# Self attention: where the next head group's transposes stand, and how its projections are spread

## The chip, the cores and the metric

The kernel runs on one core of a Trainium2 chip. Its time is that of one execution on the device in microseconds (us), as the median of several runs. A core has five engines that run their own instruction streams and wait for each other through semaphores: TensorE (matmuls, PE in the profile, with its weight loads as PEld), VectorE (DVE), ScalarE (ACT), GpSimd (POOL) and SyncE (SP, which issues DMAs here).

## The reference

A decoder block in float32 with x of shape (4, 512, 512): self attention with 16 heads of 32 and rotary embedding, cross attention to a masked context of 1601 rows, and a mixture of 16 experts with 4 chosen per token beside a shared one. Each of the three is added to its input and layer normalised. The change lies in the first:

```
q, k, v = (proj(Wq), proj(Wk), proj(Wv))          # (B, 16 heads, 512, 32)
q = q * cos + _rotate_half(q) * sin
k = k * cos + _rotate_half(k) * sin
att = jnp.einsum('bhqd,bhkd->bhqk', q, k) / math.sqrt(hd)
mask = jnp.triu(jnp.full((T, T), -jnp.inf, dtype=att.dtype), k=1)
att = jax.nn.softmax(att + mask, axis=-1)
out = jnp.einsum('bhqk,bhkd->bhqd', att, v)
out = out.transpose(0, 2, 1, 3).reshape(B, T, D)
return out @ Wo.T
```

## The kernel before

Everything in self attention is written out by hand, engine by engine, with semaphores. The work comes in 16 head groups (counter g): 4 batches times 4 groups of 4 heads. Matmuls keep near float32 accuracy by splitting each operand into a high part in the fast fp32r format and a low part, the difference; a product is then three passes, or the two parts are stacked along the contraction.

One group g on TensorE, in this order:

1. Transposes (L519): 32 of them turn the rotated query and key parts of 4 heads into `proj_ps`, 4 for each of 8 halves (query and key of head 0, of head 1, ...). `proj_ps` has 4 banks, so from the fifth half on they wait for copies of earlier ones. ScalarE copies the query halves to `q_st` (L257), VectorE the key halves to `k_st` (L378).
2. Scores, in 8 steps of two heads (L471, and L473 which adds the causal mask); VectorE takes the row maximum of each (L387). Two PSUM banks hold scores, so a score waits for the maximum of the one two before it. Behind each step stand 5 of the 48 matmuls that project x for the next group (L438). In the first group of a batch the output projection of the batch before follows (L453, 48 matmuls).
3. 4 more projections, the transposes of the negative maxima (L540), and the last 4 projections. ScalarE and VectorE copy the maxima to `q_st` (L270, L407) as further rows of the contraction.
4. Transposed scores (L487), again in 2 banks, from which ScalarE takes the exponentials into `p_t` (L278). There are 4 blocks of keys (kc) with 4 heads each. GpSimd zeroes the masked half of each diagonal square (L202), and the values (L494) and weight sums (L501) of a block follow, interleaved with the next block's transposed scores. The last block's values and sums have nothing behind which to stand.

Beside part 4 VectorE rotates the next group's queries and keys once all its projections are done. It multiplies by cosines (L317) and sines (L320) and adds (L324), first for queries and then for keys. Then it copies the key's high part (L330), the values (L333), and subtracts for the low part (L335). ScalarE writes the query's high part behind the tenth exponential (L242), GpSimd its low part behind the third block's masks (L191). VectorE finishes the output of group g - 1 between the first maxima of g (L346 to L360), and ScalarE and GpSimd split it (L249, L195).

The weights of the output projection arrive in the buffer `rows` and are split once: ScalarE's `hi_wo` (L236) stands behind group 0's exponentials, VectorE's part (L304) behind its rotation for group 1. SP loads the residual `rows` over them when that is done. Nothing of cross attention or the experts starts before self attention has ended.

Of the kernel before, what the change touches and what calls it, by code (L numbers as in the profile page):

```python
# [40 lines left out]
TT = T // P  # L41
# [19 lines left out]
def self_attention(nc, sem, rows, xT, x, wqkvT, woT, rope, gather_x1):  # L61


    with ExitStack() as ctx:
# [82 lines left out]
        def groups(body):  # L147
            for b in range(B):
                for hg in range(HG):
                    body(b, hg, b == 0 and hg == 0, b == B - 1 and hg == HG - 1)  # L150

        with nc.Block() as block:
# [71 lines left out]
            @block.scalar  # L224
            def _(act):
                def hi_x(b, i):
                    if b >= 1:
                        act.wait_ge(x_in, b * 16)
                        act.wait_ge(projected, (b * HG - 1) * TT + i + 1)
                    src, hi, _ = x_places(b, i)  # L230
                    nc.scalar.activation(hi, src, ACT.Copy).then_inc(x_hi, 1)

                def hi_wo():
                    src, hi, _ = wo_places()
                    act.wait_ge(wo_in, 16)
                    nc.scalar.activation(hi, src, ACT.Copy).then_inc(w_hi, 1)  # L236

                def hi_q(g):
                    act.wait_ge(roped, g * 6 + 3)
                    act.wait_ge(turned, g * 2 * GH)  # L240
                    src, two_hi, _, _ = split_places(0)
                    nc.scalar.activation(two_hi, twice(src), ACT.Copy).then_inc(q_hi, 1)  # L242

                def hi_out(g, hg):

                    act.wait_ge(o_scaled, g + 1)
                    if hg == 0:
                        act.wait_ge(out_proj, g)
                    nc.scalar.activation(o_sp[:, 0, hg, :], o_f[:, :], ACT.Copy).then_inc(o_hi, 1)  # L249

                def group(b, hg, first, last):
                    g = b * HG + hg

                    act.wait_ge(scored_t, g * GH * TT)
                    for h in range(GH):
                        act.wait_ge(turned, g * 2 * GH + 2 * h + 1)
                        nc.scalar.activation(q_st[0:3 * HD, h, :], proj_ps[0:3 * HD, 2 * h % 4, :],  # L257
                                             ACT.Copy).then_inc(q_stacked, 1)
                    if hg == HG - 1 and not last:
                        hi_x(b + 1, 2)  # L260
                        hi_x(b + 1, 3)
                    if not first:
                        hi_out(g - 1, (hg - 1) % HG)
                    if hg == HG - 2 and b < B - 1:
                        hi_x(b + 1, 0)
                        hi_x(b + 1, 1)

                    act.wait_ge(max_turned, g + 1)
                    for h in range(0, GH, 2):
                        nc.scalar.activation(q_st[3 * HD:P, h, :], den_ps[32 * h:32 * h + 32, :],  # L270
                                             ACT.Copy).then_inc(max_stacked_a, 1)
                    act.wait_ge(summed, g)
                    for kc in range(TT):
                        w = T - kc * P
                        for h in range(GH):
                            n = kc * GH + h
                            act.wait_ge(scored_t, g * GH * TT + n + 1)
                            nc.scalar.activation(p_t[:, h, p_at[kc]:p_at[kc] + w],  # L278
                                                 score_ps[:, n % 2, kc * P:T], ACT.Exp,
                                                 scale=float(HD) ** -0.5).then_inc(exped, 1)  # L280
                            if n == 2 * GH + 1 and not last:
                                hi_q(g + 1)
                    if g == 0:
                        hi_wo()

                for c in range(DC):
                    act.wait_ge(chunk_in[c], 32)
                    hi_x(0, c)
                    src, hi, _ = w_places(c)
                    nc.scalar.activation(hi, src, ACT.Copy).then_inc(w_hi, 1)  # L290
                hi_q(0)
                groups(group)
                hi_out(NG - 1, HG - 1)

# [128 lines left out]
            def _(pe):  # L423
# [52 lines left out]
                def scores_t(g, kc, half):  # L476

                    q0 = min(kc * P, T - 2 * P)
                    for h in range(2 * half, 2 * half + 2):
                        n = kc * GH + h  # L480
                        if kc == 0 and h % 2 == 0:
                            pe.wait_ge(max_stacked_a, g * (GH // 2) + h // 2 + 1)
                        if kc == 0 and h % 2 == 1:
                            pe.wait_ge(max_stacked_v, g * (GH // 2) + h // 2 + 1)
                        if n >= 2:
                            pe.wait_ge(exped, g * GH * TT + n - 1)
                        nc.tensor.matmul(score_ps[:, n % 2, q0:T], k_st[:, h, kc * P:(kc + 1) * P],  # L487
                                         q_st[:, h, q0:T], start=True, stop=True).then_inc(scored_t, 1)
# [14 lines left out]
                                              start=(kc == 0), stop=(kc == TT - 1))  # L503
                    return mm

                def group(b, hg, first, last):
                    g = b * HG + hg

                    pe.wait_ge(q_lo, g + 1)
                    pe.wait_ge(roped, g * 6 + 5)  # L510
# [10 lines left out]
                                                     ident_r[:, :])  # L521
                        mm.then_inc(turned, 1)

                    STEP = 5
                    for n in range(2 * TT):
                        scores(g, n // 2, n % 2)
                        if not last:
                            project(g + 1, (hg + 1) % HG, n * STEP, (n + 1) * STEP)
                    if hg == 0 and not first:
                        project_out(b - 1)  # L530
                    at = 2 * TT * STEP
                    if not last:
                        project(g + 1, (hg + 1) % HG, at, at + 4)

                    pe.wait_ge(max_lo, g + 1)
                    if hg == 0 and not first:
# [3 lines left out]
                        mm = nc.tensor.transpose(den_ps[:, qt * P:(qt + 1) * P].bitcast(F32R),  # L540
                                                 neg_max[:, qt, :, :].rearrange("p h n -> p (h n)"), ident_r[:, :])
                    mm.then_inc(max_turned, 1)
                    if not last:
                        project(g + 1, (hg + 1) % HG, at + 4, len(products))
                    pe.wait_ge(maxed, g * GH * TT + GH * TT)
                    scores_t(g, 0, 0)
                    scores_t(g, 0, 1)
                    for kc in range(1, TT):
                        scores_t(g, kc, 0)
                        values(g, hg, kc - 1)  # L550
                        scores_t(g, kc, 1)
                        weight_sums(g, kc - 1)
                    values(g, hg, TT - 1)
                    weight_sums(g, TT - 1).then_inc(summed, 1)

                pe.wait_ge(const_ready, 3)
                project(0, 0, 0, len(products))
                groups(group)
                project_out(B - 1)

# [1393 lines left out]
```

## Time and profile before

| | us |
|---|---|
| median of 3 runs | 1554.73 (1553.87 to 1555.04) |
| the profiled execution | 1557.65 |
| its span, first to last instruction | 1555.9 |
| TensorE, weight loads busy | 1388.5, 1139.0 |
| VectorE busy | 1015.6 |
| ScalarE, GpSimd busy | 645.2, 334.8 |

The profile is of one execution; sums made with its durations are compared with its own time. "Granted clock" (PEclk) is TensorE's clock as a share of 2.4 GHz; it is 1.00 or 0.50 at any time, and values between are means over a stretch. "Idle before" in brackets is how long the engine stood before an instruction, with what released it.

### The profile page before, as it was taken

What the parts mean: (1) busy time and instruction counts of PE and PEld (TensorE: products, weight loads), DVE (VectorE), ACT (ScalarE), POOL (GpSimd) and SP (SyncE); (2) the same over time, 40 slices, a digit from 0 to 9 for tenths busy, and PEclk for the clock granted to TensorE, in tenths of its full rate; (3) what the DMA queues carried; (4) which work ended last, traced back from release to release, by engine and by line L of the source; (5) the groups of instructions that cost most, each with busy time, mean ns of one, the idle gap of its engine ahead of it and who ended that gap; (6) DMA issues with size and microseconds to landing.
All of it is one profiled execution on the core that took longest, in us unless ns stands there. A gap on an engine that the chain in (4) does not pass through costs nothing. (4 is left out here: it accounts for less than half of the span.)

```text
span 1555.9 us, 24568 instructions
## 1 busy us (share of the span) xinstructions
PE 1388.5 (89%) x8837; PEld 1139.0 (73%) x8837; DVE 1015.6 (65%) x1701; ACT 645.2 (41%) x1033; POOL 334.8 (22%) x491
## 2 busy tenths in 40 slices
PE   5999999999998679999999964699999999998990
PEld 5657666675665368888888854699999999997770
DVE  6767575577667275564654269677777777774777
ACT  3443244234243242423333142566565665663222
POOL 0242133123122210010100000322222222222562
PEclk9999999999998779999999985799999999998995
DMA  4200000000000131222220040677788777884563
GB/s 176 109 1 28 1 1 28 1 1 1 1 1 1 49 123 61 83 88 82 88 83 24 1 150 1 252 288 270 283 281 287 284 281 280 280 283 150 168 185 140
DMA packets 62024, 190.34 MB, mean 122 GB/s; under 512 B 7160, under 2 KB 7164, under 8 KB 61184
## 3 DMA queue, kind: packets, MB, share of 16 engines
q1 hardware_dynamic: 49312, 147.93, 26.5%
q0 software_dynamic: 12640, 41.43, 8.8%
q8 instruction: 48, 0.79, 0.2%
q14 instruction: 24, 0.20, 0.0%
HBM read 156.30 MB, written 33.03 MB: 122 GB/s over the span
## 5 line engine op out<-in xcount | busy, mean ns | idle before, releaser
L1527 DVE TENSOR_TENSOR e_w_sp<-e_w_raw,e_w_sp 128x1024 fp32r<-128x1024 f32 x141 | 168.6, 1221 | 17.9 <-ACT e_w_sp L1485 11.6
L438 PE MATMUL proj_ps<-wqkv,x_sp 128*128 128x384 f32 x768 | 170.9, 355 | 10.5 <-DVE wqkv L304 10.5
L1471 POOL DMA_INDIRECT e_x_g<-x_rows,e_index x94 | 101.3, 1078 | 321.7 <-DVE e_index L1538 307.1
L984 PE MATMUL c_score_ps<-ct,x_t 128*128 128x402 f32 x768 | 159.0, 359 | 0.0
L1485 ACT ACTIVATE e_w_sp<-e_w_raw 128x1024 fp32r<-128x1024 f32 x141 | 145.3, 1058 | 14.5 <-DMA e_w_raw<-w_experts 14.3
L1003 PE MATMUL c_out_ps<-cr,weigh_t 128*128 128x512 f32 (+1 forms) x624 | 147.3, 394 | 1.4 <-DVE weigh_t L843 1.4
L984 PEld LDWEIGHTS c_score_ps<-ct,x_t 128*128 128x128 f32 x768 | 140.6, 193 | 7.1 <-issue 5.3
L1586 PEld LDWEIGHTS e_gate_ps<-e_x_t,e_w_sp 128*128 128x128 f32 x1128 | 139.5, 190 | 5.9 <-DVE e_x_t L1548 1.8
L1586 PE MATMUL e_up_ps<-e_x_t,e_w_sp 128*128 128x256 f32 x1128 | 143.3, 283 | 0.0
L1586 PE MATMUL e_gate_ps<-e_x_t,e_w_sp 128*128 128x256 f32 x1128 | 141.0, 281 | 1.4 <-DVE e_x_t L1548 1.4
L438 PEld LDWEIGHTS proj_ps<-wqkv,x_sp 128*128 128x128 f32 x768 | 131.3, 194 | 11.1 <-issue 10.8
L1612 PE MATMUL e_down_ps<-e_w_sp,e_h_sp 128*128 128x512 f32 x564 | 139.0, 396 | 0.0
L387 DVE TENSOR_REDUCE row_max<-score_ps 128x1 f32<-128x128 f32 (+3 forms) x256 | 114.4, 485 | 34.8 <-PE score_ps L473 33.8
L1003 PEld LDWEIGHTS c_out_ps<-cr,weigh_t 128*128 128x128 f32 (+1 forms) x624 | 116.1, 188 | 26.2 <-issue 1.7
L1586 PEld LDWEIGHTS e_up_ps<-e_x_t,e_w_sp 128*128 128x128 f32 x1128 | 135.0, 188 | 0.0
L202 POOL TENSOR_SCALAR_AFFINE_SELECT p_t<-p_t 128x128 f32<-128x128 f32 x256 | 80.9, 328 | 216.1 <-ACT p_t L278 213.8
L278 ACT ACTIVATE p_t<-score_ps 128x512 f32<-128x512 f32 (+3 forms) x256 | 100.2, 437 | 51.2 <-PE score_ps L487 49.1
L1612 PEld LDWEIGHTS e_down_ps<-e_w_sp,e_h_sp 128*128 128x128 f32 x564 | 102.5, 188 | 21.4
L487 PEld LDWEIGHTS score_ps<-q_st,k_st 128*128 128x128 f32 x256 | 43.2, 194 | 96.9 <-ACT p_t L278 63.9
L487 PE MATMUL score_ps<-q_st,k_st 128*128 128x256 f32 (+2 forms) x256 | 86.6, 401 | 14.4 <-ACT p_t L278 12.7
L378 DVE CAST k_st<-proj_ps 96x512 fp32r<-96x512 f32 x64 | 40.8, 682 | 88.4 <-PE proj_ps L519 88.2
L784 ACT ACTIVATE weigh_t<-c_turn_ps 128x512 fp32r<-128x512 f32 x64 | 31.3, 515 | 134.4 <-PE c_turn_ps L959 134.4
(205 smaller groups left out, 2231.8 us busy)
## 6 DMA issues: line engine op xcount, KB each, us to landing
e_w_raw<-w_experts SPq DMA_DIRECT2D x141, 512.0 KB, 5.6
y_rows<-e_y SPq DMA_DIRECT2D x47, 512.0 KB, 3.1
raw<-ctxT SPq DMA_DIRECT2D x16, 800.5 KB, 4.3
raw<-ctx_rows SPq DMA_DIRECT2D x16, 768.0 KB, 4.9
rows<-x_rows SPq DMA_DIRECT2D x1, 4096.0 KB, 12.2
x_rows<-rows SPq DMA_DIRECT2D x4, 1024.0 KB, 5.9
out<-rows SPq DMA_DIRECT2D x4, 1024.0 KB, 5.2
rows<-wqkvT SPq DMA_DIRECT2D x4, 768.0 KB, 7.3
```

Of the source, the lines that this page charges most:

```text
L202: nc.gpsimd.affine_select(out=block_of, in_=block_of, compare_op=ALU.is_ge, fill=0.0, base=0, pattern=[[1, P]], channel_multiplier=-1).the ...
L278: nc.scalar.activation(p_t[:, h, p_at[kc]:p_at[kc] + w], score_ps[:, n % 2, kc * P:T], ACT.Exp, scale=float(HD) ** -0.5).then_inc(exped, 1)
L387: nc.vector.tensor_reduce(row_max[:, qt, h:h + 1], score_ps[:, n % 2, 0:(qt + 1) * P], AX, ALU.max).then_inc(maxed, 1)
L438: mm = nc.tensor.matmul(proj_ps[:, tt, 0:GW], x_sp[:, xs, c, tt * P:(tt + 1) * P], wqkv[:, ws, c, hg * GW:(hg + 1) * GW], start=(c == 0 an ...
L487: nc.tensor.matmul(score_ps[:, n % 2, q0:T], k_st[:, h, kc * P:(kc + 1) * P], q_st[:, h, q0:T], start=True, stop=True).then_inc(scored_t, 1)
L984: mm = nc.tensor.matmul(score_ps[:, f, 0:MQ], x1_t[:, xs, c, qt * P:(qt + 1) * P], ct[:, cs, c, f * MQ:(f + 1) * MQ], start=False, stop=(c ...
L1003: mm = nc.tensor.matmul(out_ps[:, n % 2, :], weigh_t[0:k, ws, c, :], cr[0:k, cs, c, :], start=(c == 0 and m == 0), stop=(c == MC - 1 and m ...
L1471: nc.gpsimd.indirect_dma_start(x_g[:, par, half, :], None, x2_rows, bass.IndirectOffsetOnAxis(ap=index[:, par, half:half + 1], axis=0)).th ...
L1485: nc.scalar.activation(w_sp[:, par, part, 0, :], w_raw[:, par, part, :], ACT.Copy).then_inc(w_hi[part], 1)
L1527: nc.vector.tensor_tensor(w_sp[:, par, part, 1, :], w_raw[:, par, part, :], w_sp[:, par, part, 0, :].bitcast(F32), ALU.subtract).then_inc( ...
L1586: mm = nc.tensor.matmul(ps[:, par, i, :], w_sp[:, par, part, ws, at:at + P], x_t[:, par, xs, c, :], start=(c == 0 and n == 0), stop=(c == ...
L1612: mm = nc.tensor.matmul(down_ps[:, half, :], h_sp[:, par, hs, i, half * P:(half + 1) * P], w_sp[:, par, DOWN, ws, i * D:(i + 1) * D], star ...
```

## The change

On TensorE the transposes of a group become a function of their own. It is called once ahead of group 0, and then for group g + 1 ahead of the last block's values of group g instead of at the start of g + 1. The 48 projections are spread anew: 5, 5, 4, 4, 4, 5, 4, 5 behind the eight score steps instead of 5 behind each; 4 ahead of the transposes of the maxima and 4 behind them, as before; and 4 between the first and the second pair of transposed scores. On ScalarE, `hi_wo` moves from the end of group 0 to behind its query copies. No instruction is added or removed.

```diff
@@ ScalarE, group @@
+                    if g == 0:
+                        hi_wo()
                     if not first:
                         hi_out(g - 1, (hg - 1) % HG)
...
-                    if g == 0:
-                        hi_wo()
@@ TensorE @@
-                def group(b, hg, first, last):
-                    g = b * HG + hg
+                def turn_heads(g):
                     pe.wait_ge(q_lo, g + 1)
                     pe.wait_ge(roped, g * 6 + 5)
...
-                    STEP = 5
+                STEPS = (5, 5, 4, 4, 4, 5, 4, 5)
+                BEFORE_TURN, BEHIND_TURN, BETWEEN_SCORES = 4, 4, 4
...
                     for n in range(2 * TT):
                         scores(g, n // 2, n % 2)
-                        if not last:
-                            project(g + 1, (hg + 1) % HG, n * STEP, (n + 1) * STEP)
+                        project_next(STEPS[n])
                     if hg == 0 and not first:
                         project_out(b - 1)
-                    at = 2 * TT * STEP
-                    if not last:
-                        project(g + 1, (hg + 1) % HG, at, at + 4)
+                    project_next(BEFORE_TURN)
...
                     mm.then_inc(max_turned, 1)
-                    if not last:
-                        project(g + 1, (hg + 1) % HG, at + 4, len(products))
+                    project_next(BEHIND_TURN)
                     pe.wait_ge(maxed, g * GH * TT + GH * TT)
                     scores_t(g, 0, 0)
+                    project_next(BETWEEN_SCORES)
                     scores_t(g, 0, 1)
...
+                    if not last:
+                        turn_heads(g + 1)
                     values(g, hg, TT - 1)
                     weight_sums(g, TT - 1).then_inc(summed, 1)
                 pe.wait_ge(const_ready, 3)
                 project(0, 0, 0, len(products))
+                turn_heads(0)
                 groups(group)
```

On TensorE at the change from one group to the next, before:

```order
L487 MATMUL score_ps<-q_st,k_st 128x256 x2
L501 MATMUL den_ps<-p_t,ones 32x256 x4
L494 MATMUL o_ps<-p_t,v 32x128 x4
L501 MATMUL den_ps<-p_t,ones 32x128 x4
L519 MATMUL proj_ps<-ident_r,qk_sp 96x128 x32
L471 MATMUL score_ps<-k_st,q_st 128x256
```

The same place now:

```order
L486 MATMUL score_ps<-q_st,k_st 128x256 x2
L500 MATMUL den_ps<-p_t,ones 32x256 x4
L517 MATMUL proj_ps<-ident_r,qk_sp 96x128 x32
L493 MATMUL o_ps<-p_t,v 32x128 x4
L500 MATMUL den_ps<-p_t,ones 32x128 x4
L470 MATMUL score_ps<-k_st,q_st 128x256
```

The 32 transposes into `proj_ps` have gone ahead of the last block's values (`o_ps`) and sums (`den_ps`).

On TensorE where the transposed scores begin, before:

```order
L438 MATMUL proj_ps<-wqkv,x_sp 128x384 x9
L540 MATMUL den_ps<-ident_r,neg_max 128x128 x4
L438 MATMUL proj_ps<-wqkv,x_sp 128x384 x4
L487 MATMUL score_ps<-q_st,k_st 128x512 x4
L487 MATMUL score_ps<-q_st,k_st 128x384 x2
L494 MATMUL o_ps<-p_t,v 32x512 x4
```

The same place now:

```order
L437 MATMUL proj_ps<-wqkv,x_sp 128x384 x9
L548 MATMUL den_ps<-ident_r,neg_max 128x128 x4
L437 MATMUL proj_ps<-wqkv,x_sp 128x384 x4
L486 MATMUL score_ps<-q_st,k_st 128x512 x2
L437 MATMUL proj_ps<-wqkv,x_sp 128x384 x4
L486 MATMUL score_ps<-q_st,k_st 128x512 x2
L486 MATMUL score_ps<-q_st,k_st 128x384 x2
L493 MATMUL o_ps<-p_t,v 32x512 x4
```

Four projections have come between the two pairs of 512 columns; they are the group's last.

On ScalarE in group 0, before:

```order
L257 ACTIVATE q_st<-proj_ps 96x512 x4
L270 ACTIVATE q_st<-den_ps 32x512 x2
L278 ACTIVATE p_t<-score_ps 128x512 x4
L278 ACTIVATE p_t<-score_ps 128x384 x4
L278 ACTIVATE p_t<-score_ps 128x256 x2
L242 ACTIVATE qk_sp<-qk_cos 128x16x64
L278 ACTIVATE p_t<-score_ps 128x256 x2
L278 ACTIVATE p_t<-score_ps 128x128 x4
L236 ACTIVATE wo<-rows 128x2048
L257 ACTIVATE q_st<-proj_ps 96x512 x4
```

The same place now:

```order
L257 ACTIVATE q_st<-proj_ps 96x512 x4
L236 ACTIVATE wo<-rows 128x2048
L272 ACTIVATE q_st<-den_ps 32x512 x2
L280 ACTIVATE p_t<-score_ps 128x512 x4
L280 ACTIVATE p_t<-score_ps 128x384 x4
```

The split of the output weights (`wo`) has gone from the end of the group to behind the query copies.

## Rows read from the trace of the kernel before

**Rows 1.** Stretches: length, then busy us (and instructions) of each engine, clock, DMA.

```profile
118.31:129.38 11.07, 11.07 (x70) 9.41 (x69) 9.06 (x21) 1.34 (x3) 3.81 (x3) 1.00 0.26 96
0.00:538.00 538.00, 486.19 (x3328) 330.74 (x3328) 342.98 (x636) 196.95 (x406) 137.16 (x311) 0.96 0.07 25
58.58:88.01 29.43, 27.25 (x188) 18.57 (x189) 19.14 (x38) 9.78 (x22) 7.61 (x18) 0.94 0.35 144
115.85:143.68 27.83, 26.38 (x199) 17.80 (x198) 19.04 (x38) 12.23 (x27) 10.13 (x20) 1.00 0.11 39
143.68:184.47 40.79, 39.23 (x247) 27.16 (x246) 24.57 (x45) 11.19 (x25) 7.59 (x18) 0.96 0.00 1
...
393.92:433.23 39.31, 37.74 (x247) 26.84 (x246) 24.64 (x46) 11.19 (x25) 7.22 (x18) 1.00 0.00 1
```

**Rows 2.** Timeline (start, duration, instruction, idle before), groups 2 to 3.

```profile
112.11 1.27 POOL L191 TENSOR_TENSOR qk_sp<-qk_cos,qk_sp 128x512 fp32r<-128x512 f32 x1
...
113.20 0.64 PE L501 MATMUL den_ps<-p_t,ones 128*32 128x256 f32 x8
113.33 1.03 POOL L202 TENSOR_SCALAR_AFFINE_SELECT p_t<-p_t 128x128 f32<-128x128 f32 x4
...
114.42 0.43 PE L494 MATMUL o_ps<-p_t,v 128*32 128x128 f32 x8 [0.58 <-POOL p_t L202]
...
114.99 2.68 PE L519 MATMUL proj_ps<-ident_r,qk_sp 128*96 128x128 f32 x32
115.56 2.42 ACT L257 ACTIVATE q_st<-proj_ps 96x512 fp32r<-96x512 f32 x4 [1.93 <-PE proj_ps L519]
115.85 2.54 DVE L378 CAST k_st<-proj_ps 96x512 fp32r<-96x512 f32 x4 [5.93 <-PE proj_ps L519]
...
117.50 0.35 PE L471 MATMUL score_ps<-k_st,q_st 96*128 96x256 f32 x1
```

**Rows 3.** Waits from 0 to 538 us: total, times, longest.

```profile
PE o_ps L494 <- POOL p_t L202: 9.0, 16, 0.6
```

**Rows 4.** Timeline, groups 0 to 1.

```profile
54.42 1.91 ACT L236 ACTIVATE wo<-rows 128x2048 fp32r<-128x2048 f32 x1
...
56.37 2.29 DVE L304 TENSOR_TENSOR wo<-rows,wo 128x2048 fp32r<-128x2048 f32 x1 [5.54 <-ACT wo L236]
...
59.31 1.07 PE L519 MATMUL proj_ps<-ident_r,qk_sp 128*96 128x128 f32 x12 [1.72 <-DVE k_st L378]
...
60.23 0.35 PE L471 MATMUL score_ps<-k_st,q_st 96*128 96x256 f32 x1
```

**Rows 5.** The page's costliest groups: the maxima, busy us and mean ns.

```profile
L387 DVE TENSOR_REDUCE row_max<-score_ps 128x1 f32<-128x128 f32 (+3 forms) x256 | 114.4, 485 | 34.8 <-PE score_ps L473 33.8
```

**Rows 6.** Timeline, group 3, weight loads of one score step's projections.

```profile
122.06 0.83 PEld L438 LDWEIGHTS proj_ps<-wqkv,x_sp 128*128 128x128 f32 x5
```

**Rows 7.** Timeline, group 3, start of the transposed scores.

```profile
131.17 0.71 PE L487 MATMUL score_ps<-q_st,k_st 128*128 128x512 f32 x2
...
131.88 0.69 DVE L317 TENSOR_TENSOR qk_cos<-proj_ps,cos_t 128x512 f32<-128x512 f32 x1
...
132.48 0.95 PE L487 MATMUL score_ps<-q_st,k_st 128*128 128x512 f32 x2 [0.60 <-ACT p_t L278]
...
133.21 0.69 DVE L324 TENSOR_TENSOR qk_cos<-qk_cos,qk_sin 128x512 f32<-128x512 f32 x1
...
133.66 0.78 POOL L202 TENSOR_SCALAR_AFFINE_SELECT p_t<-p_t 128x128 f32<-128x128 f32 x2 [0.47 <-ACT p_t L278]
...
134.50 1.06 PE L494 MATMUL o_ps<-p_t,v 128*32 128x512 f32 x8
...
135.13 0.69 DVE L324 TENSOR_TENSOR qk_cos<-qk_cos,qk_sin 128x512 f32<-128x512 f32 x1
135.16 0.82 POOL L202 TENSOR_SCALAR_AFFINE_SELECT p_t<-p_t 128x128 f32<-128x128 f32 x1 [0.19 <-ACT p_t L278]
```

**Rows 8.** Timeline, group 0, transposes at the stage's start.

```profile
27.30 3.44 PE L519 MATMUL proj_ps<-ident_r,qk_sp 128*96 128x128 f32 x32 [6.57 <-DVE v L333]
```

More of the change, by code:

```diff
@@ L522, in group, with project_next @@
                         mm.then_inc(turned, 1)
-                    STEP = 5
+                STEPS = (5, 5, 4, 4, 4, 5, 4, 5)
+                BEFORE_TURN, BEHIND_TURN, BETWEEN_SCORES = 4, 4, 4
+                assert sum(STEPS) + BEFORE_TURN + BEHIND_TURN + BETWEEN_SCORES == len(products)
+                def group(b, hg, first, last):
+                    g = b * HG + hg
+                    done = 0
+                    def project_next(n):
+                        nonlocal done
+                        if not last:
+                            project(g + 1, (hg + 1) % HG, done, done + n)
+                        done += n
                     for n in range(2 * TT):
                         scores(g, n // 2, n % 2)
-                        if not last:
-                            project(g + 1, (hg + 1) % HG, n * STEP, (n + 1) * STEP)
+                        project_next(STEPS[n])
                     if hg == 0 and not first:
                         project_out(b - 1)
-                    at = 2 * TT * STEP
-                    if not last:
-                        project(g + 1, (hg + 1) % HG, at, at + 4)
+                    project_next(BEFORE_TURN)
                     pe.wait_ge(max_lo, g + 1)
@@ L552, in group @@
                         weight_sums(g, kc - 1)
+                    if not last:
+                        turn_heads(g + 1)
                     values(g, hg, TT - 1)
```

## The prediction

> **What bounds the kernel now.** I read the page's first part, then a table of stretches, then the waits, then the timeline where one head group ends and the next begins. Self attention fills the first 538 us of a span of 1555.9 us [rows 1], and all later stages start behind its end, so what it gives back should reach the end one for one. In that stretch TensorE is busy 486 of 538 us, VectorE 343, ScalarE 197, GpSimd 137 [rows 1]. A steady group (start of its key copies to the next one's) takes 27.83 us at granted clock 1.00, with 26.38 us of TensorE in it [rows 1]: TensorE sets the pace and is idle in small gaps. The reader should see three of them. At a group's end it stands 0.58 us until GpSimd has masked the last block [rows 2], and that wait recurs in all 16 groups, 9.0 us in all [rows 3]. Behind the first two transposed scores it stands 0.60 us for an exponential [rows 7]. Between groups 0 and 1 it stands 1.72 us inside the transposes, since VectorE is then splitting the output weights [rows 4]. Where the clock fell, a group cost more: group 1 took 29.43 us instead of 27.83, and of the groups with an output projection one took 40.79 instead of 39.31 [rows 1]; one more of each kind is like them, so four groups of 15.
>
> **Transposes ahead of the last values.** In the steady change of groups the last but one weight sums end at 113.84 (113.20 + 0.64), the values wait until 114.42, the transposes start at 114.99, the next scores at 117.50 [rows 2]. Nothing is added, only the order changes. The moved transposes wait for the low query part, which GpSimd ends at 113.38 (112.11 + 1.27) [rows 2], ahead of the 113.84 where TensorE comes free. VectorE's parts end earlier: it has stood idle 5.93 us before the copies of 115.85 [rows 2]. So the transposes start near 113.8. From the third head on they wait for copies of earlier ones; those start 0.57 us (ScalarE) and 0.86 us (VectorE) after the transposes do [rows 2], and neither engine has other work by then: ScalarE's idle 1.93 us puts the last exponential's end at 113.63. So the transposes keep their 2.5 us. The masks end at 114.36 (113.33 + 1.03) [rows 2], under them, and values and sums (0.57 us from 114.42 to 114.99) follow with no wait. Scores then start at 113.8 + 2.5 + 0.57, about 0.58 us earlier. Ends of the range: 0, if a wait of equal length comes in the transposes, to 0.7. I take the whole of the wait, because every producer is done. Fourteen steady changes: 14 x 0.58 = 8.1 us.
>
> **Output weights.** ScalarE's copy of 1.91 us [rows 4] goes from the end of group 0, where it stood in front of the query copies, to behind group 0's query copies, where ScalarE waits some 6 us for the transposed maxima. VectorE's half (2.29 us, from 56.37 to 58.66 [rows 4]) then finds its input ready and runs right behind its rotation, which ends at 50.83 (56.37 less 5.54 idle [rows 4]), so it is over by 53.5, before the key copies are due. SP's load of the residual rows, which waits for it, goes out some 5 us earlier and is used 100 us later. Gone at this place: the 0.58 us wait and the 1.72 us wait [rows 4]. The clock fell behind that stall, and the group took 29.43 instead of 27.83 us [rows 1]; I count that 1.60 as gone too. Together 3.9 us (2.3 if the clock falls nevertheless).
>
> **Four projections out of the score steps.** The third, fourth, fifth and seventh step now hold four projections instead of five. Five weight loads take 0.83 us [rows 6], so one costs 0.167 and four 0.67 us of TensorE. But VectorE's maxima and the finishing of the last output lie beside it, busy 9.06 us of 11.07 [rows 1], with little left in the later steps, and a pair of scores needs the maximum taken two scores before. Stepping through the eight pairs with maxima of 0.49 us in the mean [rows 5], short for narrow scores and long for wide ones, I find the last maximum about 0.45 us earlier, the rest going into small waits. Group 0 has no output to finish and should get all of 0.67. Fourteen groups (the last has no projections): 14 x 0.45 + 0.67 = 7.0 us; ends 0 and 15 x 0.67 = 10.
>
> **The same four between the first transposed scores.** They take 4 x 0.167 = 0.67 us, beside a wait for which the first exponential is the cause: the second pair of transposed scores starts 1.31 us after the first (131.17 to 132.48), of which the matmuls take 0.71 [rows 7]. They fit, to within 0.1 us. Their cost lies elsewhere. The last of them completes the projection, and VectorE's rotation waits for that: its first multiplication would start near 132.65 instead of 131.88 [rows 7] (the four start behind the second scores near 131.65, 0.167 apart, and the last takes 0.36 to its end; reaching VectorE takes near 0.1 more). The rotation has room on its own path, since VectorE is idle 5.93 us behind it [rows 2]. But look at what GpSimd does beside it. A mask takes 0.26 to 0.29 us (four in 1.03 [rows 2]), yet the one that started at 135.16 took 0.82, and the two from 133.66 took 0.78 together; in both cases VectorE was in its addition of cosine and sine parts (135.13 for 0.69, 133.21 for 0.69) [rows 7]. So a mask stands until that addition is nearly over. With the rotation 0.77 us later the first addition covers about 133.97 to 134.65. The fourth mask of the first block becomes ready at about 134.15 and ends at 134.44 now; it would end near 134.87. The values at 134.50 wait for just this mask [rows 7], and TensorE makes nothing of it up later: of its 1.45 us of idle time in a group (27.83 less 26.38) 0.58 and 0.60 are the waits named, and it runs nearly without a gap between the first values and the last. So 0.43 us is lost in each group that rotates: 15 x 0.43 = 6.5 us. Ends: 0, if the addition starts 0.2 us later than I work out or the mask slips in first, to 15 x 0.65 = 10 when the mask meets its very start. I take 6.5.
>
> The Trainium skill has a rule for this ("GPSIMD Engine Reference", section "Key points"): GpSimd shares its SBUF interfaces with VectorE, with contention when VectorE runs in a two-port mode or reads two inputs from SBUF. The addition reads two such inputs; the multiplications ahead of it read one from PSUM, and the masks beside them kept 0.29 us. The trace agrees, and by this rule the loss stands as above; without it the sum would be 6.5 us better.
>
> **Sum.** 8.1 + 3.9 + 7.0 - 6.5 = 12.5 us. The profiled execution took 1557.65 us (1.75 us around its span), so 1545.2 profiled. It was 2.9 us above the median of 1554.73, so I predict 1542. The three other falls of the clock (about 1.5 us each, from 40.79 against 39.31 [rows 1]) I leave as they are: more matmuls stand in front of them, but TensorE now waits for the mask as well. Later stages get the same work at a shifted time; I count nothing.
>
> **Rivals.**
> Masks and additions miss each other, by a tenth or two of a microsecond. For it: the fourth mask is ready only some 0.5 us before the addition ends, and my start of the rotation is worked out, not read. Against it: the addition is 0.69 us long and must be missed whole. Time: 1542 - 6.5, about 1535.5; with the three falls of the clock gone too, 1531.
> VectorE paces the scores. Then the shorter steps give nothing: 1542 + 6.3, about 1548.5. For it: 9.06 busy of 11.07. Against it: VectorE itself starts the phase 1.2 us earlier, because its key copies move with the transposes, and the scores only 0.58.
> The wait is only handed on: the transposes stall on a copy or the low part for as long as the values did, scores and masks cancel: within 3 us of 1554.7.
> Slower: the clock falls in every change of groups. The transposes now stand directly behind the transposed-scores phase, the thinnest of the group, and the last values no longer part them. At half clock 32 transposes took 3.44 us, at the start of the stage [rows 8], against 2.68 at full clock [rows 2], 0.76 more; a fall in the phase itself costs 1.5. Fourteen groups x 2.26 = 31.6, less the 4.4 already in the sum: about 1569. It decides from six more groups on (12.5 / 2.26 = 5.5). Against it: at the steady change the clock is 1.00 [rows 1], with the same transposes and more idle time than there will be.
> The Trainium skill ("TensorE: Matmul & The Clock Gate", Part 4, PE-mode transpose) says that transposes do not bring up the full clock as other matmuls do, which speaks for this rival; here 32 of them ran in 2.68 us in a stretch at full clock, so they at least do not end it.
>
> **How the numbers follow.** Forecast 53%, masks missed 30%, VectorE paces 10%, handed on 3%, slower 4%. This kernel's measurement can tell 0.2%, 3.1 us. The first three are all faster: 93%; same 3%; slower 4%. The range holds the first three, less the far ends: 1532 to 1549.
>
> **What would show it.** The values of a last block follow the transposes with no wait for GpSimd (9.0 us of waits gone); scores start about 2.9 to 3.1 us after the second last weight sums end. The first rotation multiplication starts about 1.5 us after the first transposed scores, and a mask of the first block takes over 0.5 us, with a new wait of the first values behind it. Group 1's copies start with no stall, and its clock is 1.00. A steady group takes 27.83 - 0.58 - 0.45 + 0.43 = 27.2 us. I am wrong if steady groups take 26.8 (masks missed), 27.7 (VectorE paces), or if the clock row shows falls in more than five groups.

## The result and the profile after

The changed kernel takes 1544.37 us in the median of 4 runs (1543.84 to 1544.55), the kernel before 1554.88 (1553.87 to 1555.07): a ratio of 0.9933 with a 95% interval of 0.9916 to 0.9950. I had forecast 1542 in a range of 1532 to 1549. The profiled execution took 1544.55 us around a span of 1542.8, against 1557.65 before.

Stretches of the profile after, in the form of [rows 1]: self attention, a steady group from key copies to key copies, group 1, and one group's score phase.

```profile
0.00:522.00 522.00, 485.02 (x3328) 334.00 (x3328) 343.35 (x636) 196.96 (x406) 139.01 (x311) 0.97 0.07 26
112.53:139.69 27.16, 26.64 (x199) 18.11 (x198) 19.06 (x37) 12.22 (x27) 10.08 (x20) 1.00 0.11 40
58.12:85.33 27.21, 26.68 (x199) 18.12 (x198) 19.07 (x38) 11.20 (x25) 7.55 (x18) 1.00 0.29 126
114.85:125.40 10.55, 10.55 (x68) 8.70 (x65) 8.46 (x20) 1.46 (x3) 3.80 (x3) 1.00 0.28 101
```

Self attention ends 16 us earlier, after 522 us and not 538. A steady group takes 27.16 us instead of 27.83 and stands 0.52 us of it (27.16 less 26.64), not 1.45. Group 1 no longer costs more than the others.

The change from group 2 to group 3 in the timeline after, in answer to [rows 2]:

```profile
110.00 1.28 POOL L191 TENSOR_TENSOR qk_sp<-qk_cos,qk_sp 128x512 fp32r<-128x512 f32 x1
...
111.09 0.64 PE L500 MATMUL den_ps<-p_t,ones 128*32 128x256 f32 x8
111.23 1.02 POOL L202 TENSOR_SCALAR_AFFINE_SELECT p_t<-p_t 128x128 f32<-128x128 f32 x4
...
111.66 2.68 PE L517 MATMUL proj_ps<-ident_r,qk_sp 128*96 128x128 f32 x32
112.24 2.40 ACT L257 ACTIVATE q_st<-proj_ps 96x512 fp32r<-96x512 f32 x4 [0.71 <-PE proj_ps L517]
112.53 2.54 DVE L377 CAST k_st<-proj_ps 96x512 fp32r<-96x512 f32 x4 [4.32 <-PE proj_ps L517]
114.27 0.43 PE L493 MATMUL o_ps<-p_t,v 128*32 128x128 f32 x8
...
114.52 0.40 PE L500 MATMUL den_ps<-p_t,ones 128*32 128x128 f32 x8
...
114.85 0.38 PE L470 MATMUL score_ps<-k_st,q_st 96*128 96x256 f32 x1
```

The reader is to see that the transposes, the values and the scores follow each other without a bracket, so TensorE waits for none of them; the masks of 111.23 end at 112.25, two microseconds before the values that need them.

The start of the transposed scores of group 3 after, in answer to [rows 7]:

```profile
128.06 0.71 PE L486 MATMUL score_ps<-q_st,k_st 128*128 128x512 f32 x2
128.61 0.86 PE L437 MATMUL proj_ps<-wqkv,x_sp 128*128 128x384 f32 x4
129.38 0.96 PE L486 MATMUL score_ps<-q_st,k_st 128*128 128x512 f32 x2
129.51 0.69 DVE L316 TENSOR_TENSOR qk_cos<-proj_ps,cos_t 128x512 f32<-128x512 f32 x1 [0.76 <-PE proj_ps L437]
...
130.83 0.69 DVE L323 TENSOR_TENSOR qk_cos<-qk_cos,qk_sin 128x512 f32<-128x512 f32 x1
131.04 1.31 POOL L202 TENSOR_SCALAR_AFFINE_SELECT p_t<-p_t 128x128 f32<-128x128 f32 x3 [0.20 <-ACT p_t L280]
...
131.73 1.07 PE L493 MATMUL o_ps<-p_t,v 128*32 128x512 f32 x8 [0.26 <-POOL p_t L202]
```

The projections fit where the 0.60 us wait was. The rotation starts 1.45 us behind the first transposed scores (0.71 before [rows 7]). The fourth mask now meets VectorE's addition of 130.83, and the first values have a wait for GpSimd of 0.26 us.

The largest waits of TensorE for these lines in self attention after, where [rows 3] had 9.0 us in 16 waits:

```profile
PE o_ps L493 <- POOL p_t L202: 5.3, 17, 1.1
PE score_ps L486 <- ACT p_t L280: 3.5, 17, 0.4
```

Of the 16 waits at the groups' ends only the last group's is left, 0.29 us. The other 16 are new: 15 stand at the first values of a group (0.26 to 0.28 us each) and one of 1.1 us stands in group 0.

### The profile page after: what moved, and what is told of

It reads as the page before. It is cut to its first block and busy times, and to the rows that moved or that the text cites. A ratio compares the mean times of both kernels' runs of the same rounds, so it can differ in the third digit from the quotient of the medians.

```text
span 1542.8 us, 24568 instructions
## 1 busy us (share of the span) xinstructions
PE 1389.8 (90%) x8837; PEld 1144.5 (74%) x8837; DVE 1016.9 (66%) x1701; ACT 646.1 (42%) x1033; POOL 336.1 (22%) x491
## 5 line engine op out<-in xcount | busy, mean ns | idle before, releaser
L470 PE MATMUL score_ps<-k_st,q_st 96*128 96x256 f32 (+2 forms) x256 | 86.5, 385 | 1.8 <-DVE row_max L386 1.6
```

The lines of the kernel that those rows point to most:

```text
L470: nc.tensor.matmul(score_ps[:, n % 2, 0:wide], q_st[0:3 * HD, h, qt * P:w], k_st[0:3 * HD, h, 0:wide], start=True, stop=False)
```

## The experiments

The first three kernels do one part of the change each; on their chip the kernel before took 1554.08 us.

**The transposes alone.** Against the changed kernel, with `hi_wo` back at group 0's end:

```diff
-                STEPS = (5, 5, 4, 4, 4, 5, 4, 5)
-                BEFORE_TURN, BEHIND_TURN, BETWEEN_SCORES = 4, 4, 4
+                STEPS = (5, 5, 5, 5, 5, 5, 5, 5)
+                BEFORE_TURN, BEHIND_TURN, BETWEEN_SCORES = 4, 4, 0
```

> The kernel before with only the transposes ahead of the last values; projections 5 behind each score step and none between the transposed scores, output weights split late. By my account the wait of 0.58 us goes in each steady change of groups: period 27.83 - 0.58 = 27.25 us, time 1554.9 - 14 x 0.58 = about 1546 to 1547, the stall of group 1 mostly staying. First values wait for no mask longer than before. If the four falls of the clock inside attention went because projections now stand between the transposed scores, some falls are still there (2 to 4); if they went because the idle gap at the group's end went, there is none. Rival (the gain is from the spread): period stays 27.8, time 1554.

Measured: 1550.51 us, ratio 0.9979 (0.9970 to 0.9989); a steady group takes 27.37 us. The time is 4 us above what I expected. One reason is at the change from group 0 to group 1, where the stall did not stay as it was:

```profile
58.50 0.47 PE L517 MATMUL proj_ps<-ident_r,qk_sp 128*96 128x128 f32 x4 [0.89 <-ACT q_st L257]
...
60.95 1.51 PE L517 MATMUL proj_ps<-ident_r,qk_sp 128*96 128x128 f32 x12 [1.98 <-DVE k_st L377]
```

The transposes come earlier, but ScalarE and VectorE are still splitting the output weights, so TensorE stands 2.87 us in them and not 1.72 [rows 4]. The granted clock is at its half level from 60.3 us on, for twice as long as in any fall of the kernel before. The late split of the weights costs more once the transposes have moved.

**The spread projections alone.** The transposes back at the group's start, `hi_wo` back too:

```diff
                 def group(b, hg, first, last):
                     g = b * HG + hg
+                    turn_heads(g)
...
-                    if not last:
-                        turn_heads(g + 1)
                     values(g, hg, TT - 1)
```

> The kernel before with only the new spread of the projections. Mine: scores end 0.4 to 0.5 us earlier, the first values wait 0.33 us for a mask held by VectorE's addition, so a period of 27.7 us, time 1553 with the falls of the clock as before, 1549 if filling the gap between the transposed scores is what removes them. If the mask's delay comes from the transposes instead, the first values don't wait here and the period is 27.4. Rival (the spread gives nothing or costs): period 27.8 or more, four falls.

Measured: 1549.87 us, ratio 0.9975 (0.9965 to 0.9986); a steady group takes 27.68 us.

**The output weights alone.** Both edits above together, with `hi_wo` behind group 0's query copies.

> The kernel before with only the early split of the output weights on ScalarE. Mine: the stall of 1.72 us between groups 0 and 1 goes and with it the fall of the clock in group 1 (1.6 us), but VectorE's part of the split (2.3 us, two inputs from SBUF) now runs beside the third block's masks of group 0 and holds them, about 1.1 us on TensorE: 1554.9 - 2.2 = 1552.7 (1552 to 1554). Rival (masks held by something else in the changed kernel, such as the late rotation): no mask over 0.5 us in group 0's third block, 1551.5.

Measured: 1554.77 us, ratio 1.0007 (0.9997 to 1.0017): no change that can be told, where I expected 1552 to 1554. A group from key copies to key copies in the three (the transposes, the projections, the weights alone), then group 0 of the third:

```profile
117.49:144.86 27.37, 26.50 (x199) 17.87 (x198) 19.24 (x37) 12.22 (x27) 10.17 (x20) 1.00 0.11 39
```

```profile
115.88:143.56 27.68, 26.57 (x199) 18.03 (x198) 18.84 (x38) 12.24 (x27) 10.11 (x20) 1.00 0.11 39
```

```profile
115.21:143.05 27.84, 26.39 (x199) 17.80 (x198) 19.04 (x38) 12.22 (x27) 10.14 (x20) 1.00 0.12 39
...
29.53:59.54 30.01, 27.71 (x200) 19.07 (x198) 19.64 (x35) 12.18 (x25) 8.13 (x17) 0.94 0.15 53
```

In the steady groups the parts add up: 0.46 for the transposes and 0.15 for the projections, 0.61 of the 0.66 that both give together. In the medians they do not: 3.6 and 4.2 us, less 0.7, are 7.1, and the whole change gives 10.5. The longer stall of the transposes alone and the falls of the clock, which differ between the kernels, lie in between; no run divides the rest. Nor has any run the transposes and the projections without the early split, so what the split is worth beside them is not measured.

Group 0 takes 30.01 us, as long as in the kernel before (30.00, 58.58 less 28.58), although the stall of 1.72 us [rows 4] has gone. Two things hide that. The first is the clock. These rows show group 0 up to its first transposed scores and from there to group 1's first scores, in the kernel before and then in this one:

```profile
28.58:44.25 15.67, 15.67 (x108) 13.49 (x106) 10.79 (x24) 2.54 (x6) 0.00 (x0) 0.95 0.00 1
44.25:60.23 15.98, 12.81 (x114) 6.32 (x113) 10.30 (x14) 11.18 (x23) 6.33 (x17) 1.00 0.12 32
```

```profile
29.53:46.15 16.62, 16.62 (x108) 14.31 (x106) 10.98 (x24) 4.34 (x7) 0.00 (x0) 0.89 0.00 1
46.15:61.19 15.04, 12.74 (x112) 6.31 (x113) 10.30 (x14) 9.34 (x22) 8.13 (x17) 1.00 0.37 141
```

The first part is 0.95 us longer, at a mean clock of 0.89 and not 0.95: the stage starts with a stretch at half clock, which here reaches 3.8 us into group 0 and in the profile of before 1.6 us. It begins anywhere between 23.2 and 26.7 us in the 14 profiled executions (26.5 here, 23.3 in before). It is not the weights: the transposes alone, with the late split, take 16.59 us for this part at 3.75 us of half clock. The second part is 0.94 us shorter. That is what the early split gives, of the 1.72 us. The timeline shows what took the rest:

```profile
52.65 2.29 DVE L303 TENSOR_TENSOR wo<-rows,wo 128x2048 fp32r<-128x2048 f32 x1
52.89 2.93 POOL L202 TENSOR_SCALAR_AFFINE_SELECT p_t<-p_t 128x128 f32<-128x128 f32 x4 [0.71 <-ACT p_t L280]
...
55.87 0.64 PE L493 MATMUL o_ps<-p_t,v 128*32 128x256 f32 x8 [0.85 <-POOL p_t L202]
```

VectorE's subtraction for the weights reads two inputs from SBUF for 2.29 us. The mask started beside it ends behind it: four masks take 2.93 us, not 1.03, and the values come 0.85 us late. The same place in the changed kernel:

```profile
52.46 3.18 POOL L202 TENSOR_SCALAR_AFFINE_SELECT p_t<-p_t 128x128 f32<-128x128 f32 x4 [0.56 <-ACT p_t L280]
...
52.61 2.38 DVE L303 TENSOR_TENSOR wo<-rows,wo 128x2048 fp32r<-128x2048 f32 x1
...
55.69 0.64 PE L493 MATMUL o_ps<-p_t,v 128*32 128x256 f32 x8 [1.09 <-POOL p_t L202]
```

In the changed kernel the values wait 1.09 us. About half of the stall was moved from the transposes to the masks.

**The additions behind the multiplications.** To test the price of the mask, the rotation does its four multiplications first (they read PSUM) and its two additions then, behind the fourth mask; ScalarE's high query part waits for the first addition at its new place:

```diff
                     for s in range(2):
                         ...
+                    for s in range(2):
-                        dve.wait_ge(roped, g * 6 + 3 * s + 2)
+                        dve.wait_ge(roped, g * 6 + 2 * s + 2)
```

> The changed kernel, with VectorE's rotation in another order: all four multiplications first, then the two additions. No instruction added. Mine: the fourth mask of the first block now lies beside multiplications that read PSUM and takes 0.29 us, the first values follow the transposed scores with no wait: period 27.17 - 0.33 = 26.85, time 1544.4 - 15 x 0.33 = about 1539.5. Rival (the mask is late because the exponential or TensorE is late, or any VectorE work holds it): the mask still takes over 0.5 us or starts late, period 27.17, time 1544.

Measured: 1535.65 us, ratio 0.9884 (0.9866 to 0.9902). Its timeline at the same place:

```profile
128.64 0.30 POOL L202 TENSOR_SCALAR_AFFINE_SELECT p_t<-p_t 128x128 f32<-128x128 f32 x1 [0.20 <-ACT p_t L280]
...
129.00 1.06 PE L494 MATMUL o_ps<-p_t,v 128*32 128x512 f32 x8
...
129.51 1.38 DVE L324 TENSOR_TENSOR qk_cos<-qk_cos,qk_sin 128x512 f32<-128x512 f32 x2
129.66 0.68 POOL L202 TENSOR_SCALAR_AFFINE_SELECT p_t<-p_t 128x128 f32<-128x128 f32 x1 [0.19 <-ACT p_t L280]
```

The fourth mask takes 0.30 us, the first values wait for nothing, and the collision falls on a mask of the second block, which nobody waits for. A steady group takes 26.86 us, 0.31 less than in the changed kernel. So the mask's price is shown: 15 x 0.31 = 4.7 us. The kernel gained more than that, 8.7 us against the changed one (7.5 against its repeat), each measured on another chip. From the first rotation's first multiplication to the first key copies it takes 6.90 us (21.08 to 27.98) and not 7.75 (21.50 to 29.25): in the changed kernel the second addition took 1.75 us beside GpSimd's subtraction for the low query part, and here both additions are over, in 1.28 us, before that subtraction starts. Cross attention takes 3 us less, of which more below.

The next three shared a chip on which the kernel before took 1553.34 us.

**The changed kernel again**, with one more execution of before in the profile:

> The changed kernel once more, unchanged, as a second profile and as the time beside which the next two stand. Mine: steady groups again 27.17 us and no fall of the clock between groups 1 and 14; in cross attention the part behind the stage's start again 2 to 3 us longer than before the change if VectorE's split of the context rows again meets GpSimd's mask bias from the wrong side, 0 if that order is chance. Time 1544.4, or 1542 in the second case.

> The kernel before once more, for a second profile. Mine: steady groups 27.83 us to 0.01, but another number of falls of the clock than the four of the first profile: the runs of before differ by 3 us and this profile was 2.9 us above their median, about two falls. So 1 to 3 falls. Rival (the falls belong to fixed groups): groups 1, 4, 7 and 8 again.

Measured: 1543.16 us, ratio 0.9934 (0.9917 to 0.9951), and one execution of before at 1554.06. The gain is the same as the first time.

**The output weights in four pieces**, each 512 columns wide, between the maxima of group 0, where GpSimd has nothing that TensorE waits for:

```diff
+                            if first and n % 2 == 1 and 1 <= n // 2 <= HG:
+                                lo_wo(n // 2 - 1)
...
-                    if g == 0:
-                        lo_w(DC, wo_places())
```

> The changed kernel with VectorE's split of the output weights cut in four and put between the maxima of group 0, where no mask is due. Mine: the masks of group 0's third block take 0.29 us each again instead of standing 2.4 us behind the one long subtraction, the key copies of group 1 come 1.1 to 1.8 us earlier, less 0.3 us for the maxima pushed back: time 1.0 to 1.5 us below the changed kernel. Rival (the hold in group 0 is not from this instruction): same time, same late masks.

Measured: 1541.39 us, ratio 0.9924 (0.9907 to 0.9940), 1.8 us under the changed kernel beside it, though the two intervals overlap. In its profile group 0 takes 27.77 us (28.87 and 28.42 in two looks at the changed kernel), and the waits have gone:

```profile
54.04 0.57 POOL L202 TENSOR_SCALAR_AFFINE_SELECT p_t<-p_t 128x128 f32<-128x128 f32 x2 [0.87 <-ACT p_t L280]
...
54.66 0.64 PE L499 MATMUL o_ps<-p_t,v 128*32 128x256 f32 x8
```

**Both together:**

> The changed kernel with both: additions behind all four multiplications, and the output weights split in four pieces between group 0's maxima. Mine: the two act in different places and add: steady groups 26.86 us, group 0 shorter by 1 to 1.5 us, 1535.6 - 1.2 = about 1534.4; up to 2 more where cross attention's order of mask bias and split falls the other way.

Measured: 1535.96 us, ratio 0.9889 (0.9873 to 0.9906). Its group 0 takes 27.10 us and its steady groups 26.85, but the median is no better than with the additions alone on another chip; the 1.3 us of group 0 (28.42 less 27.10) can't be told from no change. Beside the pieces alone, on the same chip and with cross attention's order (below) alike in both profiles, the additions give 5.4 us (1541.39 less 1535.96). That is the 4.7 of the masks and the 0.85 (7.75 less 6.90) of the start.

**Cross attention's mask bias.** By the profiles self attention gives back 16.0 us, the whole kernel 13.1. Some 2 us of the rest go in cross attention, as this stretch of the changed kernel's timeline shows:

```profile
564.53 5.61 POOL L770 TENSOR_SCALAR mask_bias<-mask_u 1x1608 bf16<-1x1608 uint8 x1 [32.40 <-DMA mask_u<-mask]
565.08 5.19 DVE L849 TENSOR_TENSOR cr<-raw,cr 128x1536 fp32r<-128x1536 f32 x1 [0.58 <-ACT cr L786]
...
570.93 0.66 PE L963 MATMUL c_turn_ps<-c_ident,rows 128*128 128x128 f32 x4 [0.74 <-DVE weigh_t L854]
```

and the same in the kernel before, where VectorE came 0.01 us first:

```profile
580.01 1.76 DVE L838 TENSOR_TENSOR cr<-raw,cr 128x1536 fp32r<-128x1536 f32 x1 [0.58 <-ACT cr L775]
580.02 7.22 POOL L759 TENSOR_SCALAR mask_bias<-mask_u 1x1608 bf16<-1x1608 uint8 x1 [31.68 <-DMA mask_u<-mask]
```

From the first to the last of its scores, cross attention takes 320.6 us in the profile of before and 322.9 in that of after. The last experiment lets GpSimd wait, so that the two can't meet:

```diff
                     pool.wait_ge(mask_in, b * 16 + 16)
+                    if b == 1:
+                        pool.wait_ge(*split(0, LOADS - 1))
```

> The version with the rotation's additions behind its multiplications and the output weights in pieces, and one edit more: GpSimd's mask bias for batch 1 of cross attention waits until VectorE has split the last part of the context, so it can't be under way when VectorE takes the parts of the first keys. Theory that the two engines exclude each other there and that whoever starts first holds the other up: both operations last as long as alone (the bias about 5.6 us, VectorE's split about 1.8 us, not 5.2), in every execution. In the version without the edit the split already came first in its profiled execution, so the profile shows the same order and its time is the same within 1 us: about 1535 in the median, 1532.5 to 1533.5 of span; its runs should scatter less downwards from 1537. Rival, that the order of the two is worth nothing to the end: same time. Rival, that the wait only delays the bias until it is late for the second batch: slower by some us, with a wait of TensorE or VectorE for GpSimd in cross attention.

> The additions behind the multiplications and the output weights in pieces once more, to be compared with the version with the later mask bias on one chip. Expected 1536 in the median (1534 to 1537), steady groups of 26.86 us, group 0 of 27.1 us, no fall of the granted clock in the attention's groups. Theory that GpSimd and VectorE meet by chance in cross attention: some runs 2 us longer than others.

Measured, side by side: 1547.07 us with the wait (ratio 0.9886, 0.9870 to 0.9903), 1546.28 without (0.9885, 0.9869 to 0.9902), on a chip where the kernel before took 1564.68 us; all kernels profiled there spent 12 to 16 us more in the shared expert, their last stage, than on the earlier chips. In the version with the wait VectorE's fourth split of the batch's context rows takes 1.76 us, in the one without 4.75:

```profile
559.23 1.76 DVE L858 TENSOR_TENSOR cr<-raw,cr 128x1536 fp32r<-128x1536 f32 x1 [0.24 <-ACT cr L795]
...
564.55 5.61 POOL L779 TENSOR_SCALAR mask_bias<-mask_u 1x1608 bf16<-1x1608 uint8 x1 [39.64 <-DVE cr L858]
```

```profile
556.68 7.06 POOL L777 TENSOR_SCALAR mask_bias<-mask_u 1x1608 bf16<-1x1608 uint8 x1 [31.86 <-DMA mask_u<-mask]
...
559.12 4.75 DVE L856 TENSOR_TENSOR cr<-raw,cr 128x1536 fp32r<-128x1536 f32 x1 [0.25 <-ACT cr L793]
```

So the two instructions exclude each other here, as the theory had it, but the first rival was right about the end: where VectorE's third split (that of 565.08 and of 580.01 above) comes first, its fourth can be held for 3 us and nobody is late (320.7 us of cross attention in both). What costs is the bias ahead of the third split: the four profiled executions in which it was (after, its repeat, the repeat of before, the transposes alone) show it each time, and take 322.1 to 322.9 us for this stretch, against 319.6 to 320.7 in the ten others. No experiment forced the bad order, so its price rests on that comparison.

**The clock, looked at again.** Two kernels once more, on the same chip:

> Only the transposes ahead of the last block's values, a second execution with a profile. Theory A, that the clock falls go because the four projections fill the gap between the first transposed scores: without them in this kernel at least one fall in the groups between 0 and 15 (the first execution had one double fall, at group 1's stall). Theory B, that they go because the last values no longer stand alone at the group's end, so that the transposes alone suffice: at most the one at group 1's stall, as before. Theory C, that falls vary from one execution to the next whatever the kernel: a number between 0 and 4 at other places than the first time. About 1550.5 us, steady groups of 27.37 us.

> Only the projections spread anew, a second execution with a profile. Theory A, that four projections between the first transposed scores keep the clock up: no fall in the groups between 0 and 15, as in the first execution. Theory B, that the transposes' place does: falls as in the kernel before, two to four. Theory C, that falls vary from one execution to the next whatever the kernel: one or more is as likely as none. About 1550 us, steady groups of 27.68 us.

Measured: 1559.71 and 1560.96 us, one execution each, on the chip with the slower shared expert. Three stretches of self attention in [rows 1]'s form, of this second look at the transposes alone and then at the spread projections alone; the figure to read is the granted clock, third from the end:

```profile
38.00:78.00 40.00, 36.27 (x237) 24.45 (x235) 26.74 (x48) 13.98 (x27) 7.53 (x18) 0.91 0.26 106
78.00:278.00 200.00, 193.77 (x1406) 131.86 (x1405) 138.30 (x264) 81.47 (x175) 62.92 (x134) 1.00 0.03 12
278.00:470.00 192.00, 186.13 (x1290) 127.74 (x1288) 129.50 (x245) 70.92 (x152) 49.97 (x112) 0.99 0.00 1
```

```profile
38.00:78.00 40.00, 36.64 (x248) 24.64 (x247) 29.24 (x53) 17.31 (x33) 9.61 (x24) 1.00 0.27 106
78.00:278.00 200.00, 192.62 (x1399) 132.82 (x1396) 132.94 (x260) 78.32 (x168) 60.93 (x128) 1.00 0.03 12
278.00:470.00 192.00, 185.07 (x1288) 128.32 (x1286) 126.06 (x241) 71.63 (x153) 50.93 (x114) 1.00 0.00 1
```

Counted over all profiled executions between 38 and 470 us: with projections between the transposed scores no fall to the half clock in nine executions of six kernels; without them at least one in each of five (before 4 and 2, the transposes alone one of double length and then 3, the weights alone 1). The falls' places and their number vary from one execution to the next, so the third theory is right in part; that they come only without those projections speaks for the first. It does not prove it: the same edit takes four projections out of the score steps, and no run separates the two halves.

## Why the prediction held, and where it did not

**The transposes:** mechanism right, size 0.46 and not 0.58 us. All producers were done, as I had said. From the start of the last but one sums to the scores it now takes 3.76 us (111.09 to 114.85) against 4.30 [rows 2], which is 0.54. The rest goes later, in the score steps (12.47 us from the first scores to the maxima's transposes in the transposes alone, 12.38 before); what takes it I can't name. 14 x 0.46 = 6.4, not 8.1.

**The score steps:** right. The spread projections alone shorten the steps by 0.40 us and the maxima's transposes by 0.08, together 0.48 where I had 0.45. VectorE does not pace them. Group 0 did not get all of 0.67, though it has no output to finish: at nearly the same stretch of half clock (3.9 and 3.75 us) its part up to the transposed scores takes 16.13 us after and 16.59 in the transposes alone, 0.46 less.

**The mask:** right in place and sign, 0.34 and not 0.43 us. I had the rotation start 1.48 us behind the first transposed scores, and it is 1.45. The first values come 3.67 us behind those scores (128.06 to 131.73), where it was 3.33 (131.17 to 134.50 [rows 7]). The mask met the addition 0.21 us behind its start, nearly as worked out (0.18), but ended 0.15 us behind it, not 0.22. I also read one row wrongly: of the two masks from 133.66 only the first was held, for 0.40 us, and the 0.78 has a gap in it. The Trainium skill ("GPSIMD Engine Reference", section "Key points") names this contention; the trace agrees, and the kernel with the additions behind gives its price, 0.31 us in a group. Its time, 1535.65, is near what I had for the rival in which mask and addition miss each other (1535.5), but only half of the gain over the changed kernel comes from the masks, so that nearness is luck.

The three make 0.66 us in a steady group (0.46 + 0.48 - 0.34 = 0.60 by the parts); I had 27.2 us, and it is 27.17; the errors of 0.12 and 0.09 us in two of the parts had opposite signs. In the three groups with an output projection the gain is 0.59 us (39.31 to 38.72), so the fourteen give 11 x 0.66 + 3 x 0.59 = 9.0 us.

**The output weights:** the step that failed. I wrote that VectorE's half "then finds its input ready and runs right behind its rotation", and stopped at whether VectorE had time. It had, but GpSimd has the third block's masks beside it. Of the 1.72 us the weights alone give 0.94, and in the changed kernel the values wait 1.09 us for those masks. I expected 2.5 us from group 0 (0.58 + 1.72 + 0.67 - 0.43). From its first key copies to group 1's first scores it gave 0.5 (31.65 to 31.19). Of the missing 2.1, about 1.0 went to the masks (1.1 in the third block, 0.1 less than expected in the first) and 0.2 is missing from the score steps. The other 0.9 is chance and not the change: the stretch at half clock at the stage's start reached 2.3 us further into the group. From key copies to key copies the group gave 1.1 (30.00 to 28.87), since group 1's copies now also stand ahead of the last values.

**The clock:** group 1's fall went, 1.6 us as counted. The three others, which I had left as they were, went too, 4.6 us. I took a mask's wait for a reason that they would stay; the looks at the parts speak for the filled gap between the transposed scores, without proving it.

**Later stages:** not nothing. They took 2.9 us more, of which about 2 by the order of two instructions in cross attention. Another 0.9 lies behind cross attention's scores (682.4 us to the end, 681.5 before) and is absent from the repeat (681.5), so it is scatter. The order is no fixed effect of the change either: the repeat of before has the bad one too. The start of self attention took 0.7 more (0.1 in the repeat) and its last group gave 0.3.

So the profiled difference is 9.0 + 1.1 + 1.6 + 4.6 + 0.3 - 0.7 - 2.9 = 13.0 us (13.1 measured), where I had 12.5. That it is nearly right is luck: three falls outside my sum gave 4.6, while group 0 gave less and the later stages took 2.9. Between the medians it is 10.5. I took off 2.9 us because before's profiled execution was that far above its median. But that surplus was at least in part its falls (4 against 2 in the second look, at 1554.06 us and on another chip), and after has none to take off; the changed kernel's profiled time and median are 0.2 us apart. Without that correction the forecast would have been 1545.2.

The slower rival is refuted: in the changed kernel no group at its change shows a fall, with 32 transposes standing directly behind the transposed scores.

## What to carry to other kernels

When a wait is removed by moving work, check the engine that shares memory with the mover and not only the one that waits: here two terms hung on what GpSimd did beside a two-input VectorE instruction, and putting the additions behind the masks and the multiplications gained 5.4 us on one chip, about half of what the whole change gives. A correction from the profiled run to the median holds only if the change leaves alone what made that run slow. A stage whose length the change doesn't touch can still move by microseconds when two instructions there change their order.

## What the runs showed of the hardware

In every meeting read here of a GpSimd instruction and a VectorE instruction with two inputs in SBUF, the one that started second ended only behind the first, and it worked in both directions. A 0.29 us mask that started 0.21 us behind an addition of 0.69 us ended 0.15 us behind it, one that started 0.24 us behind a 2.29 us subtraction took 2.20 us, and a VectorE subtraction of 1.76 us took 5.19 beside GpSimd's conversion of 1x1608 bytes, which ran 5.61 us on one partition. When VectorE was first by 0.01 us, GpSimd's took 7.22 us and VectorE's its 1.76. Beside VectorE's multiplications, with one input in PSUM, the masks kept their 0.29 us.

The granted clock's falls are not a property of a place in the program: the same kernel had four in one execution and two in another, and only the one at 61 us, behind the stall of group 1's transposes, at the same place.
